# Gathered table rows placed in h's own storage by an unrolled GpSimd program

## The reference

```python
h = jnp.concatenate([x[row], edge_attr], axis=1)
h = jax.nn.relu(_bn(h @ W1 + b1, g1, be1))
s = jax.ops.segment_sum(h, col, num_segments=n)
cnt = jax.ops.segment_sum(jnp.ones((h.shape[0], 1), h.dtype), col, num_segments=n)
agg = jnp.where(cnt > 0, s / jnp.maximum(cnt, 1.0), 0.0)
h2 = jnp.concatenate([x, agg], axis=1)
h2 = jax.nn.relu(_bn(h2 @ W2 + b2, g2, be2))
out = jax.nn.relu(h2 @ Wl + bl)
x = _layernorm(x + out, axis=-1)
```

## Time and profile before

| | us |
|---|---|
| median of three timed runs | 901.51 |
| lowest, highest | 897.14, 904.6 |
| span of the profiled execution, first to last instruction | 892.4 |
| median less this span (the page gives the profiled execution's span alone) | 9.1 |
| stage 1, table and lists | 52 |
| stage 2, edge loop | 676 |
| stage 3, all after it | 164 |

### The profile page before, as it was taken

One profiled execution on the slowest core, in us unless ns is written; L12 is line 12 of the kernel. 1 busy time (PEld: TensorE's weight loads), 2 busy tenths in 40 slices (PEclk: granted clock), 3 DMA queues, 4 the chain that ended last, 5 costly groups with the idle time before them and its releaser, 6 DMA issues.

```text
span 892.4 us, 11876 instructions
## 1 busy us (share of the span) xinstructions
PE 455.6 (51%) x2195; PEld 345.1 (39%) x2195; DVE 389.9 (44%) x905; ACT 235.3 (26%) x595; POOL 461.4 (52%) x572
## 2 busy tenths in 40 slices
PE   1644454535525455334544543354543349999662
PEld 1622232323323233223332332232332239998542
DVE  1343434334333343333434433244433267776495
ACT  0111122212212122111322222121221135655264
POOL 2046666566665655556666655565655543333352
PEclk9955555555555555555555555555555558999887
DMA  1233322223323222223332322232322224777202
GB/s 64 86 89 88 92 87 80 88 79 94 100 85 88 76 88 88 69 84 94 92 94 76 96 77 77 82 98 72 94 85 71 85 89 131 210 223 226 90 1 72
DMA packets 65229, 83.87 MB, mean 94 GB/s; under 512 B 19159, under 2 KB 44168, under 8 KB 65217
## 3 DMA queue, kind: packets, MB, share of 16 engines
q1 hardware_dynamic: 40529, 39.49, 15.2%
q0 software_dynamic: 13312, 27.29, 11.2%
q10 hardware_dynamic: 11376, 16.97, 5.2%
HBM read 63.61 MB, written 20.08 MB: 94 GB/s over the span
## 4 chain that ended last, share of the span: by engine, by line
another core or an unknown queue 30%; PE 26%; issue 16%; DMA 7%; ACT 6%; DVE 5%; POOL 3%; SPq 2%; ACTq 2%; DVEq 2%; POOLq 1%
PE psH L715 12%; PE psT L709 3%; DMA res<-spill 3%; PE psH L770 3%; PE psC L770 3%; POOL work L597 3%; ACT work L846 2%; ACT res L863 2%; DMA res<-in_x 2%; SPq L404 2%; PE psH L695 1%; PE psC L725 1%; ACTq L857 1%; DMA work<-ytab,idx 1%
## 5 line engine op out<-in xcount | busy, mean ns | idle before, releaser
L597 POOL DMA_INDIRECT work<-ytab,idx x416 | 398.7, 958 | 320.5 <-DVE idx L992 143.3
L715 PE MATMUL psH<-w1e,work 128*128 128x256 f32 x416 | 214.7, 671 | 350.0 <-ACT work L846 254.4
L715 PEld LDWEIGHTS psH<-w1e,work 128*128 128x128 f32 x416 | 121.6, 322 | 409.8 <-ACT work L846 278.1
L1052 DVE TENSOR_TENSOR work<-psH,work 128x512 f32<-128x512 f32 x104 | 71.9, 691 | 235.8 <-remote 104.7
L846 ACT ACTIVATE work<-psT 128x256 f32<-128x256 f32 x104 | 39.9, 384 | 474.2 <-remote 326.2
L1066 DVE TENSOR_TENSOR psX<-work,psX 128x512 f32<-128x512 f32 x104 | 72.1, 693 | 116.7 <-ACT work L861 76.2
L1152 DVE TENSOR_TENSOR work<-res,psX 128x512 f32<-128x512 f32 x103 | 70.7, 688 | 26.5 <-PE psC L770 12.4
L861 ACT ACTIVATE work<-work 128x512 f32<-128x512 f32 x104 | 65.3, 627 | 60.3 <-issue 33.2
L1059 DVE TENSOR_TENSOR psS<-work,psS 128x512 f32<-128x512 f32 x104 | 71.7, 689 | 2.4 <-issue 2.4
L709 PE MATMUL psT<-ident,work 128*128 128x128 f32 x208 | 68.0, 430 | 8.5 <-DMA work<-in_edge_attr 7.7
L617 POOL TENSOR_TENSOR agg<-agg,srci 128x64 f32 x104 | 32.3, 310 | 66.2 <-ACT srci L910 64.5
(11 more groups left out here) (144 smaller groups left out, 336.0 us busy)
## 6 DMA issues: line engine op xcount, KB each, us to landing
work<-in_edge_attr SPq DMA_DIRECT2D x103, 128.0 KB
work<-ytab,idx POOLq DMA_INDIRECT x416
hot_dram<-hotb ACTq DMA_DIRECT2D x26, 256.0 KB
spill<-work ACTq DMA_DIRECT2D x26, 256.0 KB
res<-spill SPq DMA_DIRECT2D x25, 256.0 KB, 2.9
hotb<-hot_dram SPq DMA_DIRECT2D x13, 256.0 KB, 3.9
work<-hot_dram SPq DMA_DIRECT2D x13, 256.0 KB, 3.2
h2x_dram<-agg ACTq DMA_DIRECT2D x25, 125.0 KB
```

Source lines behind the costliest of these rows:

```text
L597: pool.indirect_dma_start(yg[:, q % 2, j * F:(j + 1) * F], None, ytab, bass.IndirectOffsetOnAxis(ap=idx[:, q, j:j + 1], axis=0)).then_inc( ...
L715: last = pe.matmul(psH[q % 2][:, b * 2 * F:(b + 1) * 2 * F], eat[:, q % 2, b * P:(b + 1) * P], w1e[:, :, :].rearrange("p a f -> p (a f)"), ...
L1052: dve.tensor_tensor(hs[:, q % 2, :], psH[q % 2][:, :], yg[:, q % 2, :], ALU.add).then_inc(h_ready, 1)
```

## The change

- The staging tiles `yg`, `hs` and `idx` go. A gathered row lands where h will stand: in `res` for q < 3, and for q = 3 in one tile `away`, from which it is spilled. `make_h` adds psH to it in place.
- ScalarE no longer copies h to `res`; it only squares it.
- VectorE no longer stages indices; the gathers read their column of `srci` in place, at a fixed address. For that GpSimd's program is written out: 26 x 4 groups with no loop.
- A gather of group g waits for h of group g - 4 (before: g - 2). For q = 3 it also waits until the last spill has landed and until the squares and the sum of that h have been made. The first gather of the last step waits for the last `x_product`, since its place overlaps the turned x.
- `gathered` has four semaphores, one per q. `make_h` waits for the product and the rows alone.
- `x_product` and `x_product_out` move from the end of a step to behind q = 1, and the wait for `x_out` from q = 0 of the next step to the counts of q = 2 of the same.

```diff
@@ -91,8 +91,7 @@
         GF = TILES * F
         res = sb("res", [P, NI * KEEP * GF])
         work = sb("work", [P, 6, GF])
-        yg = work[:, 0:2, :]
-        hs = work[:, 2:4, :]
+        away = work[:, 0, :]
         sq = work[:, 4:6, :]
         mx = work[:, 0:4, :]
         back = work[:, 4, :]
@@ -105,7 +104,6 @@
         agg = sb("agg", [P, NAGG])
         cnt = sb("cnt", [P, NAGG])
         srci = sb("srci", [P, TILES, NG], I32)
-        idx = sb("idx", [P, U, TILES], I32)
         loc = sb("loc", [P, TILES, NG])
         basei = sb("basei", [1, NG], I32)
         ident = sb("ident", [P, P])
@@ -223,14 +221,12 @@
         ea_turned = sem("ea_turned")
         eat_ready = sem("eat_ready")
         prod_ready = sem("ea_product_ready")
-        idx_staged = sem("idx_staged")
-        gathered = [sem(f"gathered{i}") for i in range(2)]
+        gathered = [sem(f"gathered{i}") for i in range(U)]
         h_ready = sem("h_ready")
         sq_ready = sem("sq_ready")
         h_summed = sem("h_summed")
         sq_summed = sem("sq_summed")
         s_folded = sem("sums_folded")
-        kept = sem("kept")
         spilled = sem("spilled")
         hotb_ready = sem("hotb_ready")
         cnt_ps = sem("cnt_psum_ready")
@@ -301,6 +297,10 @@
 
             return res[:, bass.ds((i * KEEP + q) * GF, GF)]
 
+        def slot(i, q):
+
+            return resg(i, q) if q < KEEP else away
+
         def sq_fold(k):
 
             return sq[:, 0, k * F:(k + 1) * F]
@@ -588,20 +588,27 @@
             pool.drain().then_inc(s_set, 1)
             pool.wait_ge(s_tab, TAB)
 
+            pool.wait_ge(s_idx, 1)
+
             def gather(i, q):
-                if not first(i, q, 2):
-                    pool.wait_ge(h_ready, U * i + q - 1)
-                pool.wait_ge(idx_staged, U * i + q + 1)
-                pool.sem_inc(slot_passed, 1)
+
+                g = U * i + q
+                if g >= U:
+                    pool.wait_ge(h_ready, g - U + 1)
+                if q == KEEP and i:
+                    pool.wait_ge(spilled, 16 * i)
+                    pool.wait_ge(sq_ready, g - U + 1)
+                    pool.wait_ge(h_summed, g - U + 1)
+                if i == NI - 1 and q == 0:
+                    pool.wait_ge(x_ps, NT)
+                rows = res[:, (i * KEEP + q) * GF:(i * KEEP + q + 1) * GF] if q < KEEP else away
                 for j in range(TILES):
                     pool.indirect_dma_start(
-                        yg[:, q % 2, j * F:(j + 1) * F], None, ytab,
-                        bass.IndirectOffsetOnAxis(ap=idx[:, q, j:j + 1], axis=0)
-                    ).then_inc(gathered[q % 2], 16)
-
-            for q in range(U):
-                gather(0, q)
-            with pool.Fori(1, NI) as i:
+                        rows[:, j * F:(j + 1) * F], None, ytab,
+                        bass.IndirectOffsetOnAxis(ap=srci[:, j, g:g + 1], axis=0)
+                    ).then_inc(gathered[q], 16)
+
+            for i in range(NI):
                 for q in range(U):
                     gather(i, q)
 
@@ -728,20 +735,21 @@
 
             def x_product(i):
 
-                pe.wait_ge(cnt_added, U * i + U - 1)
+                pe.wait_ge(cnt_added, U * i + 1)
                 for h in range(H2):
                     last = pe.matmul(psC[0][:, h * PN:(h + 1) * PN], w2x[:, h * P:(h + 1) * P],
                                      xt0[:, bass.ds(i * PN, PN)], start=True, stop=True)
                 last.then_inc(x_ps, 1)
 
             def edge_step(i):
+                turned_out = not (isinstance(i, int) and i == NI - 1)
                 for q in range(U):
                     product(i, q)
-                    if q == 0 and not (isinstance(i, int) and i == 0):
-                        pe.wait_ge(x_out, i)
+                    if q == 2 and turned_out:
+                        pe.wait_ge(x_out, i + 1)
                     counts(i, q)
-                if not (isinstance(i, int) and i == NI - 1):
-                    x_product(i)
+                    if q == 1 and turned_out:
+                        x_product(i)
 
             edge_step(0)
             with pe.Fori(1, NI - 1) as i:
@@ -845,22 +853,19 @@
                     act.wait_ge(prod_ready, g - 1)
                 act.activation(eat[:, q % 2, :], psT[q % 2][:, 0:2 * P], ACT.Copy).then_inc(eat_ready, 1)
 
-            def store(i, q):
+            def squares(i, q):
 
                 g = U * i + q
                 act.wait_ge(h_ready, g + 1)
                 if q == KEEP:
-                    act.dma_start(spill[bass.ds(i, 1), :, :].rearrange("a p f -> (a p) f"), hs[:, q % 2, :]
-                                  ).then_inc(spilled, 16)
+                    act.dma_start(spill[bass.ds(i, 1), :, :].rearrange("a p f -> (a p) f"), away).then_inc(spilled, 16)
                 elif q == KEEP - 1:
                     act.wait_ge(hotb_ready, U * i + U)
                     act.dma_start(hot_dram[bass.ds(i, 1), :, :].rearrange("a p w -> (a p) w"),
                                   hotb[:, :, :].rearrange("p q w -> p (q w)")).then_inc(hot_saved, 16)
                 if not first(i, q, 2):
                     act.wait_ge(sq_summed, g - 1)
-                act.activation(sq[:, q % 2, :], hs[:, q % 2, :], ACT.Square).then_inc(sq_ready, 1)
-                if q < KEEP:
-                    act.activation(resg(i, q), hs[:, q % 2, :], ACT.Copy).then_inc(kept, 1)
+                act.activation(sq[:, q % 2, :], slot(i, q), ACT.Square).then_inc(sq_ready, 1)
 
             def x_product_out(i):
 
@@ -877,9 +882,9 @@
                         turned(i, q + 1)
                     elif not (isinstance(i, int) and i == NI - 1):
                         turned(i + 1, 0)
-                    store(i, q)
-                if not (isinstance(i, int) and i == NI - 1):
-                    x_product_out(i)
+                    squares(i, q)
+                    if q == 1 and not (isinstance(i, int) and i == NI - 1):
+                        x_product_out(i)
 
             act.wait_ge(s_idx, 1)
             turned(0, 0)
@@ -987,10 +992,6 @@
                 dve.tensor_copy(xtv[:, t0:t0 + n, :], psC[b % 2][:, 0:n * PN].rearrange("f (t p) -> f t p", t=n)
                                 ).then_inc(s_xt, 1)
 
-            def stage_idx(i, q):
-
-                dve.tensor_copy(idx[:, q, :].unsqueeze(2), srci[:, :, bass.ds(U * i + q, 1)]).then_inc(idx_staged, 1)
-
             turned_x(0)
             turned_x(1)
 
@@ -1008,8 +1009,6 @@
                 turned_x(b)
             dve.wait_ge(s_rowt, 3)
             link(dve.tensor_copy(srci[:, :, :].rearrange("p j g -> p (j g)"), psS[:, 0:TILES * NG]))
-            for q in range(U):
-                stage_idx(0, q)
             dve.wait_ge(s_cols, 16 * 6)
             for a in range(2):
                 last = dve.tensor_tensor(w1e[:, a, :], w1e[:, a, :], sgn, ALU.mult)
@@ -1041,22 +1040,15 @@
             def make_h(i, q):
                 g = U * i + q
                 dve.wait_ge(prod_ready, g + 1)
-                dve.wait_ge(gathered[q % 2], 64 * (2 * i + q // 2 + 1))
-                if not first(i, q, 2):
-                    dve.wait_ge(h_summed, g - 1)
-                    dve.wait_ge(sq_ready, g - 1)
-                    if q == 1:
-                        dve.wait_ge(spilled, 16 * i)
-                    else:
-                        dve.wait_ge(kept, {0: 3 * i, 2: 3 * i + 1, 3: 3 * i + 2}[q])
-                dve.tensor_tensor(hs[:, q % 2, :], psH[q % 2][:, :], yg[:, q % 2, :], ALU.add).then_inc(h_ready, 1)
+                dve.wait_ge(gathered[q], 64 * (i + 1))
+                dve.tensor_tensor(slot(i, q), psH[q % 2][:, :], slot(i, q), ALU.add).then_inc(h_ready, 1)
 
             def sum_h(i, q):
                 g = U * i + q
                 dve.wait_ge(h_ready, g + 1)
                 if not first(i, q, 1):
                     dve.wait_ge(h_summed, g)
-                dve.tensor_tensor(psS[:, :], hs[:, q % 2, :], psS[:, :], ALU.add).then_inc(h_summed, 1)
+                dve.tensor_tensor(psS[:, :], slot(i, q), psS[:, :], ALU.add).then_inc(h_summed, 1)
 
             def sum_sq(i, q):
                 g = U * i + q
@@ -1073,8 +1065,6 @@
             def edge_step(i):
                 for q in range(U):
                     make_h(i, q)
-                    if not (isinstance(i, int) and i == NI - 1):
-                        stage_idx(i + 1, q)
                     if q < U - 1:
                         onehot_b(i, q + 1)
                     elif not (isinstance(i, int) and i == NI - 1):
@@ -1155,7 +1145,6 @@
                 for q in range(U):
                     maxes(i, q)
 
-            dve.wait_ge(kept, NI * KEEP)
             wide = dve.value_load(rowi[0:1, 0:1], min_val=0, max_val=N)
             with dve.If(wide < WIN):
                 sum_step(0)
```

## The result

| | before | after |
|---|---|---|
| median of the runs compared, us | 901.45 (897.14 to 904.6, 4 runs) | 913.14 (910.54 to 916.23, 4 runs) |
| ratio, 95% interval | | 1.0139 [1.0092, 1.0185] |
| profiled execution: time, span | not given, 892.4 | 916.23, 914.5 |
| edge loop, stage 3 | 676, 164 | 698, 164.5 |

What follows compares the result with a forecast made beforehand. POOL's gathers, its waits on two row tiles and starvation of TensorE and VectorE bound the edge loop. 901.5 - 10 (four groups ahead) - 6 (fewer waits) = 885.5, said as 885 us; range 862 to 893, for 8 in 10 768 to 928.

Steps and rivals of the forecast that it cites:

- Starvation: Edge loop: back-to-back gathers leave TensorE's completions and VectorE's control steps trickling after 5 to 10 us, until gathers drain.
- Four groups ahead: Edge loop: cycles carry five groups instead of four, mean 6.40 us a group against 6.5; -10 us, bounds -149 to +39.
- New waits of the gathers: Gathers of q = 3 wait for the last spill: 0, three groups being ready ahead; at worst 26 x 2.8 = +73 us.
- Rival B: Edge loop: starvation sets the pace, longer trains feed it; all cycles 27.5 us, +39 us, 940; half, 920; chance 0.22.
- Fewer waits: `make_h` and POOL drop waits; 0.3 us on each of about 26 cycles where VectorE crawls: -6 us, bound -39.
- copies: Edge loop: dropping VectorE's index copies (20.5 us) and ScalarE's h copies (48.0 us) each valued at 0.
- add in place: VectorE's add for h: same engine, size and operand kinds, 104 x about 0.69 us before and after; 0.
- x_product: TensorE's product moved from behind q = 3 to behind q = 1: same work, 0; at most +35 us if ScalarE is late.
- Written-out program: POOL's gathers without a loop: 0, bounds 62 us to either side.
- The estimate of 65 us: VectorE's index copies lock GpSimd out; if every fourth met a gather, 26 x 2.5 = 65 us more; not adopted.
- Rival A: Edge loop: POOL alone is the bound, held back by two row tiles; 753 us, or 803; chance 0.2.
- 901.5 as the profiled execution's own time: Starting point of the sum: 892.4 us of span and 9.1 around it, taken as the profiled execution's time.

Runs made afterwards that it cites:

- e3: Changed kernel plus a drain: before every second group POOL waits until the rows of the group before have landed; 860.63 us, ratio 0.982.
- e10: Changed kernel with a fixed POOL pause of two 128x1024 memsets (2.25 us) before every second group; 845.36 us, ratio 0.944.
- e11: Changed kernel with a 128x256 memset before each gather, so one starts every 1.55 us; 874.24 us, ratio 0.976.
- e2: Changed kernel, but a gather waits for h of group g - 2 instead of g - 4; 891.41 us, ratio 1.019.
- e6: Kernel before, plus a wait before every second group until the rows of the group before have landed; 867.12 us, ratio 0.980.
- e12: Changed kernel with gathers two groups ahead and a wait for landed rows before every second group; 861.88 us, ratio 0.962.
- e4: Changed kernel with x_product and its copy out put back behind q = 3; 908.32 us, ratio 1.036.
- e8: Kernel before with only POOL's loop written out; 887.93 us, ratio 0.998.
- e16: The changed kernel unaltered, on a chip where the kernel before takes 751.77 us; 748.99 us, ratio 0.995.
- e13: Changed kernel with a 128x16 memset before each gather (one every 1.35 us), where the kernel before takes 754.45 us; 793.61 us, ratio 1.053.
- e17: Repeat of e13 (changed kernel, 128x16 memset before each gather), where the kernel before takes 751.77 us; 792.03 us, ratio 1.052.
- e5: Changed kernel plus a wait before every third group until the rows of the group before have landed; 854.23 us, ratio 0.957.
- e18: Changed kernel fetching rows of 256 bytes instead of 512, where the kernel before takes 751.77 us; 745.29 us, no ratio.
- e7: Changed kernel with three of every four gathers replaced by memsets of the same length; 698.35 us, no ratio.

## Why the prediction was wrong, point by point

- **Starvation.** The reading held. A pause of some 2 us every eight gathers (e3, e10) or a gather rate of one in 1.55 us (e11) removes it, and 2 to 6% of the time with it. One part of it said more than the rows do, that VectorE's own control steps crawl. Before the instruction at 340.12 VectorE waits for TensorE's counts, which had started 13.4 us earlier (the line below), so its 5.08 us need no crawl. After the change the list of waits puts 78.5 us of such idle time before L1038 down to remote. Of the waits shown in rows 5 only the 1.67 us before 334.35 have no other engine behind them.

```profile
326.68 0.42 PE L725 MATMUL psC<-hotb,onesb 128*128 128x64 bf16 x4
```

- **Four groups ahead: the step that failed.** I took five groups to a cycle, "trains have 20 gathers", because rows lie ready after a drain, and got -10 us, at a mean of 6.40 us a group. The trains have 16. POOL is stopped at each q = 3, and a cycle is 4 groups in 26.62 us, 6.66 each against my 6.46 for long cycles. Short trains of 6.0 to 6.4 us a group, which my mean of 6.40 kept, vanished. Against the 6.5 of before the term is +17 us in place of -10, and some +10, beside the 11.7 of the medians, when the 7 us are taken off by which the profiled execution of before was shorter than the median. e2 shows that the depth brings it, together with the one `away` tile; how much each has of it stays open. POOL's waits came to 169 us, not the 120 that I named as the sign.
- **New waits of the gathers.** I put 0, "since three groups are ready ahead of it". That counted POOL's work ahead of the wait and not who has to end it: the spill is issued by ScalarE, behind a copy that waits for starved TensorE. So it stood in every restart: 3.42 us from issue to the gather. The gap didn't grow by it (6.47 us against 7.60), but it stopped POOL at q = 3 each time, which is what holds every train to 16. That my price of 2.8 us for a landing came near is partly luck: the wait in the earlier trace rows that I took it from is put down to remote, and whether rows or TensorE's product ended it is open. What a second `away` tile would bring was not tried.
- **Rival B came true**, its mechanism and its condition: all cycles long, four groups each, a loop over 685 us (698), ScalarE's wait grown. Its price was too high: I took the 27.5 us of one cycle of before, and the cycles are 26.62, since the gap is 6.5 to 6.7 us and not 7.60. Even its lower case, 920 us if half of the cycles grow, lies above the 913 measured. Its chance, 0.22, was too low: rows 7 had shown each longer cycle to be dearer per group.
- **Fewer waits, copies, add in place.** Valued at -6 and 0. The -6 rested on the crawl of VectorE, above. e6 against e3 gives some 6 to 9 us for all parts together where nothing starves, e12 none of it to depth. Under starvation no gain is seen: e2, which has them all, is not clearly faster than the kernel before.
- **x_product.** 0 held within what e4 can tell. **Written-out program:** 0 held (e8).
- **The index copies and the gathers.** The longest gather took 1192 ns with the copies and 1205 without, the median 955 both times. They had not held it. The estimate of 65 us from the Trainium skill ("SBUF — State Buffer", the box on how VectorE blocks a DMA, and the figures below it) fell. It took the 2.5 us of the page's example for a copy of any length. The page's GpSimd is held while VectorE's copy runs, and these copies run 0.2 us, so this trace hardly tests the rule.
- **Rival A** was wrong for the chip of the result. I had worked out 753 us for the changed kernel with POOL alone as the bound; on e16's chip it takes 748.99. But there the kernel before takes 751.77 already, so A's cause, that two row tiles hold POOL back, is wrong there too: what held it back was the starvation, and the change is worth 0.5%. A profile of one chip could not have told this.
- **901.5 as the profiled execution's own time** was wrong by some 7 us, as told above.

## What to carry to other kernels

When other engines stop while GpSimd issues indirect DMAs back to back, more room for GpSimd makes it worse: hold the gathers back (here 2.25 us after every eight, 5.6%) and check that waits on "remote" vanish. A deeper prefetch is worth something only if the depth was what the engines at the bound waited for; ask of each new wait which engine ends it and what that engine is waiting for at the time. And before such a pacing is kept, time it on several chips: where nothing starves, spacing the gathers cost 5% (e13, e17) while the unpaced kernel stood at 752.

## What the runs showed of the hardware that I had not expected

- Two kinds of chip, as it looks: one program (the kernel before) takes 891 to 901 us by its medians on some and 752 to 754 on others; a gather's median is 955 ns after the change and 952 in e16. What differs stays open, and since each chip was used once, so does whether it is the chip or what went on around it at the time.
- Starvation depends on the rate of the gathers: with one in 1.26 us and pauses of 1.24 us after every eight it is there, with 2.25 us of pause or one in 1.55 us it isn't. By the mean over a cycle the limit lies between 1.43 us a gather (e5) and 1.50 (e10); an even spacing between 1.26 and 1.55 was not run where it starves. Whether bytes or the issuing count is open too, since e13 to e18 fell on chips that don't starve. Memsets in place of three gathers of four starve nobody (e7).
- What comes late is TensorE's work or its signal: transposes started at 316.90 reached ScalarE at 331.19, counts started at 316.78 reached VectorE at 331.08, with the 16 DMA engines at 0.19 of their time.
